# A graph network's kernel: the channel-major copy of the next graphs' x made by VectorE block turns and a DRAM scratch instead of TensorE transposes

## The reference, cut to what matters

```python
h = x
for i in range(L):
    hw = einsum('bnc,cd->bnd', h, weight[i])
    m = einsum('bjn,bjd->bnd', adj, hw)      # adj: 8 x 1024 x 1024
    h = gru_cell(m, h, w_ih[i], w_hh[i], b_ih[i], b_hh[i])
out = layernorm(x + h * mask)
```

## Time and profile before

| | |
|---|---|
| median of three runs | 557.03 us (553.2, 557.03, 558.19) |
| the profiled execution | 555.42 us |
| its span, first to last instruction | 553.6 us |
| mean granted TensorE clock | 0.986 |
| PE busy | 520.9 us, 94% |
| DVE busy | 436.6 us, 79% |
| ACT busy | 354.3 us, 64% |
| POOL busy | 213.7 us, 39% |
| moved by DMA | 80.93 MB, mean 146 GB/s |

### The profile page before, as it was taken

How to read it: one execution, slowest core, us unless ns; L and a number is a source line. 1 busy time by engine, 2 the same in 40 slices (tenths; PEclk the granted TensorE clock), 3 DMA queues, 4 the chain that set the end, 5 groups by cost and what they waited for, 6 DMA issues and landing times.

```text
span 553.6 us, 7447 instructions
## 1 busy us (share of the span) xinstructions
PE 520.9 (94%) x2288; PEld 420.8 (76%) x2288; DVE 436.6 (79%) x737; ACT 354.3 (64%) x568; POOL 213.7 (39%) x161
## 2 busy tenths in 40 slices
PE   5898999999999999999999999999999999999970
PEld 4576888888887888788887888778887788888850
DVE  3998767666988898876888988887688788896566
ACT  3866777648776766756876676745876775444423
POOL 0133333333265333233265532324355632334332
PEclk9999999999999999999999999999999999999985
DMA  7952355345722267365561156535580223323312
GB/s 227 387 205 76 130 189 196 113 130 175 281 81 78 66 215 234 96 186 166 182 226 57 43 205 222 156 96 174 169 292 32 74 76 115 102 68 115 95 39 80
DMA packets 79808, 80.93 MB, mean 146 GB/s; under 512 B 3656, under 2 KB 63648, under 8 KB 79776
## 3 DMA queue, kind: packets, MB, share of 16 engines
q1 hardware_dynamic: 79504, 80.41, 43.9%
q10 hardware_dynamic: 272, 0.13, 0.1%
HBM read 60.08 MB, written 20.45 MB: 145 GB/s over the span
## 4 chain that ended last, share of the span: by engine, by line
PE 31%; DVE 30%; ACT 12%; issue 11%; DMA 9%; POOL 5%; SPq 2%; DVEq 1%; POOLq 0%; ACTq 0%
PE p_S L472 13%; DMA low<-bounce 6%; ACT work L664 4%; DVE work L1108 4%; ACT adj_hi L609 4%; DVE y L919 4%; DVE work L1114 4%; DVE hT_lo L815 3%; DVE hT L931 3%; DVE S_lo L815 3%; POOL work L1231 2%; POOL work L1227 2%; PE p_r L483 2%; PE p_r L485 2%; PE p_r L484 2%
## 5 line engine op out<-in xcount | busy, mean ns | idle before, releaser
L1227 POOL TENSOR_TENSOR work<-hT,work 128x512 f32<-128x512 f32 x63 | 83.3, 1323 | 286.0 <-ACT work L664 286.0
L472 PE MATMUL p_S<-adj_hi,nat_hi 128*128 128x512 f32 x480 | 187.5, 391 | 0.0
L472 PE MATMUL p_S<-adj_hi,nat_lo 128*128 128x512 f32 x480 | 187.1, 390 | 0.0
L472 PEld LDWEIGHTS p_S<-adj_hi,nat_hi 128*128 128x128 f32 x480 | 90.1, 188 | 18.6
L472 PEld LDWEIGHTS p_S<-adj_hi,nat_lo 128*128 128x128 f32 x480 | 90.2, 188 | 18.4
L1231 POOL TENSOR_TENSOR work<-work 128x512 f32<-128x512 f32 x63 | 89.6, 1423 | 4.9
L664 ACT ACTIVATE work<-work,bias 128x512 f32<-128x512 f32 x63 | 45.5, 722 | 63.8 <-DVE work L1114 60.1
L1108 DVE SCALAR_TENSOR_TENSOR work<-p_hn,bias,work 128x512 f32<-128x512 f32 x62 | 46.5, 749 | 48.9 <-ACT work L664 48.5
L872 DVE STREAM_TRANSPOSE work<-hT 128x512 f32<-128x512 f32 x62 | 69.1, 1114 | 2.1
L609 ACT ACTIVATE S_hi<-p_S 128x512 fp32r<-128x512 f32 x64 | 37.9, 592 | 49.9 <-PE p_S L472 45.1
L931 DVE TENSOR_TENSOR hT<-work 128x512 f32<-128x512 f32 x63 | 43.2, 685 | 26.7 <-POOL work L1231 26.7
(11 more groups left out here) (149 smaller groups left out, 919.7 us busy)
## 6 DMA issues: line engine op xcount, KB each, us to landing
adj_in<-in_adj_dram SPq DMA_DIRECT2D x64, 512.0 KB, 6.5
bounce<-work SPq DMA_DIRECT2D x62, 256.0 KB, 2.0
low<-bounce SPq DMA_DIRECT2D x62, 256.0 KB, 2.8
x_in<-in_x_dram SPq DMA_DIRECT2D x8, 512.0 KB, 5.9
y<-in_x_dram SPq DMA_DIRECT2D x8, 512.0 KB, 4.2
out_dram<-y SPq DMA_DIRECT2D x7, 512.0 KB, 4.3
y<-in_L_gnn_w_ih_dram SPq DMA_DIRECT2D x2, 192.0 KB, 3.4
y<-in_L_gnn_w_hh_dram SPq DMA_DIRECT2D x2, 192.0 KB, 3.6
```

The lines of the kernel that those rows point to most:

```text
L472: last = nc.tensor.matmul(p_S[h][:, :], part[:, s, j], adj_hi[:, s, j, half(h)], start=(j == 0 and part is nat_hi), stop=(j == NB - 1 and ...
L1227: nc.gpsimd.tensor_tensor(t_sb[:, h], hT[:, s, half(h)], n_sb[:, h], ALU.subtract).then_inc(d_sub, 1)
```

## The change

All pairs but the first get hT of their x in another way. A second load of x (`load_rows`, in steps 1 and 2, with 8 consecutive nodes on a partition) fills x_in; VectorE turns it in 32x32 blocks into y (`turn_x`, two instructions of 128x512 for each graph, graph 0 in step 5 and graph 1 in step 6); SP stores y to a scratch in DRAM (`send_x`, 512 KB), and brings it back straight into hT (`bring_xT`, four DMAs of 128 KB, each to 32 partitions). Afterwards SP loads the natural x into x_in (`load_x`) and x into y (`load_y`), which therefore move. ACT's and VectorE's take_xT read hT instead of p_tr. For the pairs after the first, the TensorE transposes and the POOL sums are gone.

```diff
             def body(p, first, last):  # SP
+                    if g == 0 and not first:
+                        bring_xT(1, p)
+                    if g in (1, 2) and not last:
+                        load_rows(p, g - 1, first)
                     elif g == 4:
-                        load_y(p, 0, first)
+                        if last:
+                            load_y(p, 0, first)
                     elif g == STEPS - 2:
+                        if last:
+                            load_y(p, 1, first)
+                        else:
+                            send_x(p, 0)
+                            load_x(p, 0)
+                            next_adj(p, 1, first, range(0, 2))
+                            sp.wait_ge(x_out[0], 16 * (p + 1))
+                            load_y(p, 0, first)
+                    elif g == STEPS - 1 and not last:
+                        send_x(p, 1)
+                        load_x(p, 1)
+                        bring_xT(0, p + 1)
+                        next_adj(p, 1, first, range(2, NB))
+                        sp.wait_ge(x_out[1], 16 * (p + 1))
                         load_y(p, 1, first)
-                    elif g == 5:
-                        for s in range(2):
-                            sp.wait_ge(x_tr, 4 * p + 2 * s + 2)
-                            sp.wait_ge(xnat_lo, 2 * p + s + 1)
-                            sp.dma_start(x_in[:, s], x_v[2 * p + 2 + s]).then_inc(x_loaded[s], 16)
+            def send_x(p, s):
+                sp.wait_ge(x_turned, 4 * p + 2 * s + 2)
+                sp.dma_start(x_bounce[s], y[:, s].rearrange("p a b -> p (a b)")).then_inc(x_out[s], 16)
+            def bring_xT(s, pairs_out):
+                sp.wait_ge(x_out[s], 16 * pairs_out)
+                for q in range(Q):
+                    sp.dma_start(hT[q * 32:(q + 1) * 32, s].rearrange("r (m f) -> r m f", m=Q),
+                                 x_bounce[s].rearrange("(m r) (q f) -> q r m f", m=Q, q=Q)[q]).then_inc(x_back[s], 16)
...
             def body(p, first, last):  # TensorE
-                    if g < 2 and not (first and g == 0):
+                    if first and g == 1:
                         transpose_x(p, g, first)
...
             def turn_x(p, s, n, first):  # VectorE
+                dve.wait_ge(xrows_loaded[s], 16 * (p + 1))
+                rows = slice(n * HB, (n + 1) * HB)
+                nc.vector.transpose(y[:, s].rearrange("p a b -> p (a b)").rearrange("p (q a j) -> p j q a", q=Q, j=NB)[:, rows],
+                                    x_in[:, s, rows].rearrange("p j (q c) -> p j q c", q=Q)).then_inc(x_turned, 1)
...
+                            if g in (STEPS - 3, STEPS - 2) and not last:   # after take_back of half 1, ahead of t_mul of half 1
+                                turn_x(p, g - (STEPS - 3), 0, first)
+                    if g in (STEPS - 3, STEPS - 2) and not last:           # at the step's end
+                        turn_x(p, g - (STEPS - 3), 1, first)
...
             def body(p, first, last):  # POOL
-                    if l == 0:
+                    if l == 0 and first:
                         # hT = hT_hi + hT_lo, both halves
```

More of the change, by code:

```diff
@@ L149, in gnn_kernel @@
         x_tr = sem("x_tr")
+        xrows_loaded = [sem(f"xrows_loaded{s}") for s in range(2)]
+        x_turned = sem("x_turned")
+        x_out = [sem(f"x_out{s}") for s in range(2)]
+        x_back = [sem(f"x_back{s}") for s in range(2)]
         xT_hi = sem("xT_hi")
@@ L305, in load_y, with load_rows, load_x @@
                 sp.dma_start(y[:, s], x_v[2 * p + s]).then_inc(y_loaded[s], 16)
+            def load_rows(p, s, first):
+                if first:
+                    sp.wait_ge(x_tr, 2 * s + 2)
+                sp.wait_ge(xnat_lo, 2 * p + s + 1)
+                sp.dma_start(x_in[:, s], xrows_v[2 * p + 2 + s]).then_inc(xrows_loaded[s], 16)
+            def send_x(p, s):
[6 more added lines that the diff above has]
+                                 x_bounce[s].rearrange("(m r) (q f) -> q r m f", m=Q, q=Q)[q]).then_inc(x_back[s], 16)
+            def load_x(p, s):
+                sp.dma_start(x_in[:, s], x_v[2 * p + 2 + s]).then_inc(x_loaded[s], 16)
             def send_back(p, g, first):
@@ L339, in body @@
                     elif g == 4:
-                        if first:
-                            sp.wait_ge(start_tr, L)
-                        load_y(p, 0, first)
+                        if last:
+                            load_y(p, 0, first)
                     elif g == 5:
@@ L645, in split_x, with take_xT @@
                 copy(nat_hi[:, s], x_in[:, s]).then_inc(xnat_hi, 1)
-            def take_xT(p, s):
+            def take_xT(p, s, first):
+                if not first:
+                    act.wait_ge(x_back[s], 16 * Q * p)
+                    act.wait_ge(hn_done, HS * (p - 1) + 2 * (STEPS - 2 + s) + 2)
                 for h in range(2):
-                    act.wait_ge(x_tr, 4 * p + 2 * s + h + 1)
-                    copy(hT_hi[:, s, half(h)], flat(p_tr[h])).then_inc(xT_hi, 1)
+                    if first:
+                        act.wait_ge(x_tr, 2 * s + h + 1)
+                    copy(hT_hi[:, s, half(h)], flat(p_tr[h]) if first else hT[:, s, half(h)]).then_inc(xT_hi, 1)
             def take_back(p, g, h):
@@ L735, in body @@
                     if l == 0 and not (first and g == 0):
-                        take_xT(p, s)
+                        take_xT(p, s, first)
                     s_high(p, g, 0)
@@ L780, in _ @@
                 if j == NB - 2:
-                    take_xT(0, 0)
+                    take_xT(0, 0, True)
                 take_adj(0, 0, j)
```

16 lines of the change are left out of this document (8 added, 8 removed).

## The result

The changed kernel takes 576.58 us (median of four runs, 572.67 to 577.28); the kernel before took 556.55 us beside it (four runs, 553.2 to 558.19). The ratio is 1.0352, with a 95% interval of 1.0318 to 1.0387: 3.5% slower. The forecast was 570 us. The profiled execution of the changed kernel took 576.46 us, with a span of 574.7 us against 553.6, so 21.1 us are to be found in the trace.

A forecast was written before the change was run, and what follows sets the result against it. At pair borders the chain through VectorE, ACT and POOL was taken to pace TensorE, elsewhere 94% busy, with step 7's DMA queue full. 555.42 + 14.4 (queue) + 0.5 (turns) = 570.3, so 570 us; range 555 to 577.

The forecast's parts named there:

- rival (c): At the borders: the forecast's queue plus dear turns, slow 32-partition DMAs or low clock; 573 to 577 us, chance 0.12.
- Step 7's queue: Ahead of step 7's store: send_x, load_x, bring_xT and load_y add 6.7 us, all falling on that store.
- From the store to t_mul: Step 7 into step 0: VectorE waits 5.2 us for the load back, t_mul late; +4.8 us a border, 14.4 in all.
- Step 6: Moved loads and send_x of graph 0 in step 6: cost 0, y landing about 4 us before the residual needs it.
- The transposes: TensorE, steps 7 and 0: 48 fewer, 4.8 us of work, valued at 0 since TensorE then waits longer.
- up to 1.2 a border: TensorE's clock after standing still at each border: put at 0, up to 1.2 us if it stays low for long.
- POOL's sums: VectorE's residual of half 0 in step 0: removing the sums takes 0.44 us off the chain at each border.
- The turns: VectorE, steps 5 and 6: twelve turns of 1.1 us each, bounded by 0.75 and 2.2; 0.5 us in all.
- ACT's wait at gate r: Step 0, half 0: ACT may write at 290.5 instead of 288.39, hidden in VectorE's longer wait.
- adj blocks late on ACT: Sign against the forecast: the next graph's adj blocks come late on ACT, taken to have about 1 us.
- Rival (a): Step 7's queue: the transfers don't hold up the store, less than 1.5 us added; 554.1 us, chance 0.14.
- Rival (b): At the borders: no hold-up, and the removed TensorE work counts, 4.8 us plus 1.3 for POOL; 549.3 us, chance 0.06.

The follow-up runs named there:

- g3_late_loads: The kernel before with the loads of x_in and y of graph 1 moved into step 7; 561.63 us, ratio 1.0086.
- k2_no_bring7: The changed kernel without bring_xT of graph 0, the four DMAs to 32 partitions in step 7; 570.07 us, ratio 1.0249.
- n1_no_load6: The changed kernel without load_x of graph 0 in step 6; 574.26 us, ratio 1.0319.
- g1_path_out: The changed kernel with the whole new path left out, TensorE's transposes and POOL's sums gone as well; 556.99 us, ratio 0.9996.
- g2_no_pool_sum: The kernel before without the POOL sums of the later pairs, transposes kept; 552.87 us, ratio 0.9926.
- g4_turns_out: The changed kernel with a copy of 128 columns in place of each turn; 576.51 us, ratio 1.0361.
- k3_two_blocks_later: The changed kernel with the last two adj blocks of graph 1 behind step 7's store instead of ahead of it; 585.36 us, ratio 1.0505.
- k1_unread_transposes: g1_path_out with TensorE's 48 transposes put back as work that nobody reads; 554.14 us, ratio 0.9961.
- k4_act_copies: The kernel before with ACT copying hT whole from p_tr in steps 0 and 1 of later pairs, instead of POOL's sums; 558.45 us, ratio 1.0035.

## Why the prediction was right, and where its sizes were off

The sign, the place and the mechanism were as forecast: step 7's store behind the transfers that were put ahead of it, VectorE standing at the residual, t_mul late, TensorE waiting at p_hn. The forecast wait was 5.2 us at each border; it was 4.85, 5.01 and 4.75. The total came out 6 us above the 570, 0.4 us inside the range and in the reach of rival (c), which shares the queue's mechanism. Of the 21.7 us at the borders 18.0 stand between t_mul of step 7 and t_mul of step 0, where 14.4 were forecast; 2.5 stand ahead of it in step 7 and 1.2 behind it, and both were forecast as 0. Of (c)'s three reasons the slow 32-partition DMAs are there and the clock in part; the dear turns are not.

**Step 7's queue.** The four transfers ahead of the store were priced at 6.7 us, and the store's time thus at 2.69 + 6.7 = 9.4 us; it was 9.8, 9.6 and 11.1, mean 10.17, which is 7.5 over the kernel before. That this is so near hides errors against each other, and is luck in part. load_x and load_y were put at 1.9 each and cost 1.4 (g3_late_loads: 5.42 - 2.64 = 2.78 for both): a stretch where other things held the queue up had been taken for the rate of those loads. bring_xT was put at 1.6 and costs 2.2 (k2_no_bring7), up to 2.8 by the kernels that have the same step 7. The remainder, 7.5 - 2.8 - 2.2 = 2.5 us for send_x where 1.3 stood, is a difference, is up to 0.6 smaller with the higher price of bring_xT, and wasn't measured alone.

The runs agree with the page of the Trainium skill that the prediction weighed here. "SBUF — State Buffer", Door 1, ties DMA bandwidth to how many ports the partitions reach, and gives half of them to a transfer of 32. Here 0.524 MB to 32 partitions at a time cost 2.2 to 2.8 us of the queue, and 0.524 MB over 128 partitions 1.4 (g3_late_loads). The runs in memory are 1 KB in the first and 512 B in the second, so shorter runs are not what makes the first dearer; the source, a scratch in DRAM, is another difference that no run keeps apart.

**From the store to t_mul.** Forecast +4.8 us at each border, 14.4 in all. From t_mul of step 7 to t_mul of step 0, both of half 0, it was +5.4, +5.75 and +6.9, in all 18.0. Of the 3.6 us more, 2.5 are the store's (7.5 instead of 6.7, three times). Another 0.9 come from its issue: it follows t_mul of step 7 by 6.8 to 6.9 us before and at the first border, and by 7.35 and 7.19 at the other two, where SP has only just put out load_y when the turn is done (load_y at 286.42, the turn's end at 286.84, the store at 287.47). "SP's own issuing is no obstacle" was wrong by that much. From the load back to the end of t_mul it is 5.80, 5.86 and 5.70 us, where 5.7 were forecast.

**Step 6.** This is the step of the reasoning that failed: "0, with about 4 us to spare". It counted the load of y for the residual alone. Step 6's own store, which comes behind the new send_x, load_x, two adj blocks and load_y, wasn't looked at. It took 4.79 us at the second border and 3.56 at the third (2.27 at the first, and 2.0 at all three before), and steps 7 were 17.46 and 15.98 us. In the profile that is 2.5 us, and n1_no_load6 takes it away. Why it varies so from border to border is open; k2_no_bring7, with the same step 6, had 2.80, 3.02 and 3.27.

**The transposes.** Valued at 0, because TensorE would only wait longer. That holds for the time as far as the chain goes: at the border of g1_path_out where the clock stayed up, their removal brought nothing beyond the sums. But the longer wait has a price that was not counted: behind 1.85 us of waiting the clock fell at two borders of three, some 1.6 us each (19.18 - 17.56). In the changed kernel TensorE waits at other places, and there the low clock after the 3.47 us cost 12 matmuls 2.5 us, of which most came back in step 1, which is 0.3 to 1.1 us shorter than before and not 0.9 longer as forecast. From the end of t_mul to the next pair's step 2 it was 21.13 us at the second border against 20.46, so 0.7 was left; it was 0 at the first and 0.5 at the third. The forecast had 0, "up to 1.2 a border".

**POOL's sums.** 0.44 us a border by the residual's duration. The residual did go from 1.57 to 1.14 or 1.15 us. Alone, the removal gave 1.95 at the borders and 1.6 elsewhere (g2_no_pool_sum).

**The turns.** 1.1 us each and 0.5 in all: measured 1.168 and no difference without them (g4_turns_out). The prediction quoted the Trainium skill on this ("SBUF — State Buffer", Door 1: lines of 16 bytes, and each access that crosses to a new line pays) and took the write at 32 B as the dearer one. By the words of that rule the read at 16 B comes to a new line with each element as well, so it doesn't set the two turns apart, and no run here has a turn that is close on both sides.

**ACT's wait at gate r** was forecast as shorter than VectorE's and hidden behind it. It is there, 1.47 us, and TensorE's 1.38 at 297.94 follows from it; with VectorE free only at 300.14 it decides nothing.

```profile
288.46 1.06 ACT L639 ACTIVATE adj_hi<-adj_in 128x1024 fp32r<-128x1024 f32 x1 [1.73 <-DMA adj_in<-in_adj_dram]
...
297.12 0.69 ACT L699 ACTIVATE work<-p_r,bsum 128x512 f32<-128x512 f32 x1 [1.47 <-DMA bounce<-work]
```

The first of these two lines is what was named as a sign against the forecast: adj blocks late on ACT. They are late by 1.73 us, and at the third border by 3.12, where TensorE then stands 3.05 us before the gates of step 0 (1.73 at the second border). The "about 1 us" that they were taken to have was too much to count on. But VectorE reaches the residual all the same before the load back has landed and waits 4.75 to 5.01 us for it, so up to t_mul they add nothing here. They would show if the store came sooner: k3_two_blocks_later shows what they cost when they come later still.

**Rival (a)** would have given 554.1; the transfers are late, so it fell. g1_path_out shows that its price was off as well: without the transfers the time is 557, since the clock takes at two of three borders what POOL's sums give. **Rival (b)** fell with g1_path_out too: its transposes are gone and nothing is won by it.

## What to carry to other kernels

Before DMAs are added ahead of a store that engines wait for, add up what the queue must move up to that store. Where it was full already, each further byte, past the slack that the reader has (1.5 us here), came out as waiting of the engine that reads the result, and the other order that was tried only picked another engine (k3_two_blocks_later). Do that for every store past which a DMA is moved, not just for the fullest step. And TensorE work that fills a wait isn't free to remove: look at how long the wait becomes and at the granted clock behind it.

## What the runs showed of the hardware that I had not expected

- The borders got shorter with TensorE work that nobody reads (k1_unread_transposes): a wait of 1.82 to 1.85 us on TensorE was followed by some 3 us at a granted clock of 0.50 at two of three borders of g1_path_out, and one of 0.92 us by none. The length of the wait doesn't settle it alone: 1.84 us at the third border, and 1.73 us in step 0 of the changed kernel, were not followed by a fall.
- SP took 4.1 to 5.4 us to issue a store of 256 KB behind the full queue of the changed kernel (2.3 to 5.8 in the kernels with the same step 7), against 0.33 otherwise. In g3_late_loads, with two transfers less ahead, it was 0.33.
- A VectorE block turn that writes at a stride of 32 B and reads closely takes 1.168 us, the one that reads at 16 B and writes closely 1.114.
- Two kernels that differ only at the borders differ by 5 us outside them (k4_act_copies against the kernel before), 2.3 of it in steps whose work is the same. There the same two VectorE operations of 128x128 take 1.57 or 2.80 us, and end with the first or with the second POOL operation beside them. All 48 operations of that line together are busy for 45.5 us in the kernel before, 44.3 in g2_no_pool_sum and 51.2 in k4_act_copies.
